# A GRU and a transformer layer in one kernel: the recurrent stage's side work dealt anew to its steps

## The chip, the core and the metric

One core of a Trainium2 chip runs the whole program. The metric is the device time of one execution in microseconds (us). Three runs of the kernel before are given with their median, and one further execution was taken by the hardware profiler.

## What is computed

```python
# x: 16 x 128 x 256 (sequences, time, width), cond: 16 x 256
def cell(h, x):                       # a GRU over 128 time steps, initial state cond
    gi = x @ W_ih + b_ih
    gh = h @ W_hh + b_hh
    r = sigmoid(i_r + h_r); z = sigmoid(i_z + h_z)
    n = tanh(i_n + r * h_n)
    return (1 - z) * n + z * h
x = x + GRU(cond, x)
# a transformer layer modulated by cond: 16 heads of 128
ada = cond @ ada_w + ada_b            # shift1, scale1, gate1, shift2, scale2, gate2
x1 = layernorm(x) * (1 + scale1) + shift1
q, k, v = split(x1 @ qkv_w + qkv_b)
attn = softmax(q k^T / sqrt(128)) v
y = x + gate1 * (attn @ out_w + out_b)
x2 = layernorm(y) * (1 + scale2) + shift2
y = y + gate2 * (gelu(x2 @ ffn_w1 + ffn_b1) @ ffn_w2 + ffn_b2)
out = x + y
```

## The kernel before

The program is written out by hand, one instruction list for each engine, with semaphores between them. It has three stages: the recurrent one (the GRU), attention over 64 pairs of a head and a group of four sequences (`d`), and the feed-forward layer. Only the recurrent stage is touched by the change.

**The recurrence.** The 128 time steps are 16 blocks `r` of 8 steps `s`. All 16 sequences go together, so a step's state is a tile of 128 x 32 (two halves of the width by 16). Each step is one chain. TensorE's `gru_step` (36 matmuls, L635 and L643) multiplies the state, kept as a float16 pair `h_hi`, `h_lo`, with `W_hh`. ScalarE makes sigmoids and a tanh (L1035 to L1040), VectorE a scan (L1318), a product (L1324), the new `h_hi` (L1330), its float32 form `hs` (L1332) and `h_lo` (L1335). The next step's matmuls wait for `h_hi`.

**The side work.** Between two steps every engine does other work, in an order fixed by tables:

- TensorE's `x_bias` and `x_products` for the next block: three matmuls for the biases (L534) and 36 input products (L547), cut over the steps by the tuple `share`: at step `s` products `share[s]` to `share[s+1]`.
- *Items* of q and k made ahead for six of the heads: an item is the q or the k of one head over two finished blocks. TensorE makes it with six matmuls of 256 columns (`ahead`, L527 to L529) in bank 4, ScalarE writes `qk_hi` (`ahead_high`, L1013), VectorE `qk_lo` (`ahead_low`, L1308). All items lie in the same columns of bank 4, so an item on TensorE waits for the `qk_lo` of the item before (`qk_l`). `PART_AT` gives the steps with an item.
- The rows of the last block, normalised and modulated: `rows_sum` (L1256) adds the state to x, TensorE turns the sum (`rows_T`, L556), VectorE does `rows_stats`, `rows_var`, `rows_scale`, `rows_shift` (L1262 to L1278) with a power on GpSimd between them (`rows_rstd`, L429), TensorE turns the rows back (`rows_back`, L563), and ScalarE and VectorE write `y_hi` and `y_lo`.
- The modulation: `row_modulation` (L568, four steps of block 0) for shift1 and scale1 and eight tiles `modulation` (L576, two float32 matmuls each, written by ScalarE at L995) for the rest, at the eight steps of block 2.
- The weights of q, k and v: SyncE loads them in pieces (`load_pieces`, 512 KB each, L331), ScalarE and GpSimd split them into float16 pairs (L1002, L423).

```python
for s in range(BS):
    gru_step(r, s)
    if s == 0 and r > 0: rows_T(r - 1)
    elif s == 5 and r > 0: rows_back(r - 1)
    x_products(r + 1, products[now[s]:now[s + 1]])
    if r == MOD_AT: modulation(G1 + s)
    if (r, s) in ITEM_AT: ahead(ITEM_AT[r, s])
```

That is TensorE's loop in short (the waits left out). On VectorE the order within a step is the five instructions of the chain, then one row operation (`row_work`), then the sum, then `ahead_low`. On ScalarE, after the tanh: the high half of x, `y_high`, the modulation tile, the pieces, and last `ahead_high`.

## Time and profile before

| what | value |
|---|---|
| median of three runs | 740.95 us (738.16 to 741.0) |
| the profiled execution's own time | 741.54 us |
| its span from the first to the last instruction | 739.7 us |
| TensorE matmul busy | 711.7 us, 96% |
| VectorE busy | 575.7 us, 78% |
| ScalarE busy | 484.0 us, 65% |
| first and last start of L1330 (`h_hi`) | 11.9 and 265.1 us |
| mean granted TensorE clock | 0.986 |

The recurrent stage is the stretch from 11.9 to 265.1 us, a little over a third of the span; attention and feed-forward fill the rest. A granted clock of 1.00 is 2.4 GHz and one of 0.50 is 1.2 GHz. In a timeline each row starts with the start of the instruction in us and its duration in us. Since L1330 stands once in each step, the distance between two of its starts is the length of a step.

### The profile page before, as it was taken

To read this page: it belongs to the slowest core of one execution; us is meant where nothing else is said; L and a number is where in the kernel's file an instruction comes from. 1 tells how busy PE (TensorE), PEld (TensorE's weight loads), DVE (VectorE), ACT (ScalarE), POOL (GpSimd) and SP (SyncE) were. 2 spreads that over 40 slices of the span, in tenths; PEclk is the share of its full clock that TensorE was granted. 3 is DMA by queue.
4 is the path that set the end of the run, shared out by engine and by line. 5 is a ranking of instruction groups with operands and counts; after the bars stand their busy time and mean duration, and the time that the engine had idled before them with its cause. 6 is when DMAs were issued, how large, how long until landed. Compare 5 with 4: busy or idle time off the path is not lost.

```text
span 739.7 us, 25163 instructions
## 1 busy us (share of the span) xinstructions
PE 711.7 (96%) x10380; PEld 525.0 (71%) x10380; DVE 575.7 (78%) x1581; ACT 484.0 (65%) x1621; POOL 104.1 (14%) x134
## 2 busy tenths in 40 slices
PE   6889999999999999999999999999999999999997
PEld 5689888888888776666767667676676777644555
DVE  5667888888888878877878988888887888834643
ACT  4346666666655567776787777877777777775453
POOL 0222222222210001011001111011110111000040
PEclk9869999999999999999999999999999999999999
DMA  6311111211000302322222332223322233200001
...
DMA packets 79017, 36.70 MB, mean 50 GB/s; under 512 B 70667, under 2 KB 73911, under 8 KB 78903
## 3 DMA queue, kind: packets, MB, share of 16 engines
...
q10 hardware_dynamic: 576, 1.57, 0.6%
q14 instruction: 32, 0.26, 0.1%
...
## 4 chain that ended last, share of the span: by engine, by line
PE 83%; DVE 6%; ACT 5%; DMA 2%; SPq 2%; issue 1%; POOL 0%; DVEq 0%; ACTq 0%
PE bank L527 20%; PE bank L529 19%; PE bank L528 19%; PE bank L635 12%; PE bank L643 5%; PE bank L547 5%; SPq L381 2%; DVE h_hi L1330 2%; ACT prob L1111 1%; PE bank L534 1%; ACT zg L1037 1%; DMA pT_lo<-p_lo 1%; DVE nu L1324 1%; DMA xr<-in_weights 1%; DVE mx L1402 1%
## 5 line engine op out<-in xcount | busy, mean ns | idle before, releaser
L635 PE MATMUL bank<-h_hi,whh_hi 128*128 128x16 f16 x1536 | 111.5, 178 | 8.6 <-DVE h_hi L1330 7.2
L635 PEld LDWEIGHTS bank<-h_hi,whh_hi 128*128 128x128 f16 x1536 | 90.0, 97 | 30.2 <-DVE h_hi L1330 26.0
L635 PE MATMUL bank<-h_hi,whh_lo 128*128 128x16 f16 x1536 | 109.9, 177 | 1.5 <-issue 1.5
L1111 ACT ACTIVATE prob<-bank,nmx 128x128 f32<-128x128 f32 x256 | 90.6, 367 | 30.7 <-DVE nmx L1405 30.4
L527 PE MATMUL bank<-y_hi,w_hi 128*128 128x256 f16 (+3 forms) x344 | 108.9, 319 | 1.0 <-DVE qk_lo L1308 0.8
L529 PE MATMUL bank<-y_lo,w_hi 128*128 128x256 f16 (+3 forms) x344 | 109.1, 319 | 0.0
L528 PE MATMUL bank<-y_hi,w_lo 128*128 128x256 f16 (+3 forms) x344 | 109.1, 319 | 0.0
L635 PEld LDWEIGHTS bank<-h_hi,whh_lo 128*128 128x128 f16 x1536 | 89.7, 96 | 1.7 <-issue 1.6
L527 PE MATMUL bank<-w_hi,y_hi 128*128 128x128 f16 x512 | 89.1, 219 | 0.6 <-DVE v_lo L1409 0.6
L528 PE MATMUL bank<-w_hi,y_lo 128*128 128x128 f16 x512 | 89.1, 219 | 0.0
L529 PE MATMUL bank<-w_lo,y_hi 128*128 128x128 f16 x512 | 89.1, 219 | 0.0
L643 PE MATMUL bank<-h_lo,whh_hi 128*128 128x16 f16 x1536 | 78.6, 178 | 0.0
L1013 ACT ACTIVATE qk_hi<-bank,small 128x256 f16<-128x256 f32 (+4 forms) x96 | 44.8, 474 | 34.2 <-PE bank L529 34.2
L1104 ACT ACTIVATE p_hi<-prob 128x512 f16<-128x512 f32 x64 | 40.4, 632 | 29.5 <-DVE prob L1419 21.5
L1446 DVE TENSOR_TENSOR four<-nat,four 128x512 f16<-128x512 f32 (+1 forms) x33 | 22.7, 689 | 44.8 <-ACT four L1147 44.7
L1035 ACT ACTIVATE zr<-bank 128x32 f32<-128x32 f32 x128 | 25.6, 200 | 48.6 <-PE bank L643 44.2
L643 PEld LDWEIGHTS bank<-h_lo,whh_hi 128*128 128x128 f16 x1536 | 56.5, 96 | 0.0
L527 PEld LDWEIGHTS bank<-w_hi,y_hi 128*128 128x128 f16 x512 | 50.1, 98 | 8.1 <-DVE v_lo L1409 1.0
L1318 DVE TENSOR_TENSOR_SCAN bank<-zr,bank 128x64 f32<-128x64 f32 x128 | 37.2, 290 | 23.2 <-ACT zr L1035 21.5
L528 PEld LDWEIGHTS bank<-w_hi,y_lo 128*128 128x128 f16 x512 | 50.1, 98 | 7.1
L1402 DVE TENSOR_REDUCE mx<-bank 128x4 f32<-128x512 f32 x64 | 44.0, 687 | 13.3 <-PE bank L529 12.6
L1413 DVE TENSOR_TENSOR p_lo<-prob,p_hi 128x512 f16<-128x512 f32 x64 | 44.2, 691 | 10.2 <-ACT p_hi L1104 7.7
...
## 6 DMA issues: line engine op xcount, KB each, us to landing
...
pT_hi<-p_hi SPq DMA_TRANSPOSE x64, 2.4
pT_lo<-p_lo SPq DMA_TRANSPOSE x64, 2.4
```

What stands on the lines that cost most here:

```text
L527: mm(ps, w[0], a[0], start=start, stop=False, skip_group_check=True)
L528: mm(ps, w[1], a[0], start=False, stop=False, skip_group_check=True)
L529: return mm(ps, w[0], a[1], start=False, stop=stop, skip_group_check=True)
L547: nc.tensor.matmul(gate_cols(n, m), w[:, k, m * P:(m + 1) * P], a[:, n % 2, k, :], start=False, stop=False, skip_group_check=True)
L635: nc.tensor.matmul(out(m0 + m), half[:, k, (m0 + m) * P:(m0 + m + 1) * P], h_hi[:, k * B:(k + 1) * B, 1], start=False, stop=False, skip_gr ...
L643: mm = nc.tensor.matmul(out(m0 + m), whh_hi[:, k, (m0 + m) * P:(m0 + m + 1) * P], h_lo[:, k * B:(k + 1) * B], start=False, stop=k == KD - ...
L1013: op = nc.scalar.activation(qk_hi[:, e, part, b, t], ps, ident_f, bias=bT[:, at:at + 1])
L1104: nc.scalar.activation(p_hi[:, :], flat_prob, copy).then_inc(p_h, 1)
L1111: op = nc.scalar.activation(prob[:, j, :], bank[3][:, j * T:(j + 1) * T], ACT.Exp, bias=nmx[:, j:j + 1], scale=SCALE, accum_out=den[:, j:j ...
L1318: nc.vector.tensor_tensor_scan(npre[r % 2].rearrange("p j s -> p (j s)"), zr[:, :, :].rearrange("p j s -> p (j s)"), n_pairs[r % 2][:, :, ...
L1402: nc.vector.reduce_max(mx[:, :], bank[3][:, :].rearrange("p (j s) -> p j s", j=QUAD), AX.X).then_inc(s_mx, 1)
L1413: tt(p_lo[:, :], flat_prob, p_hi[:, :], ALU.subtract).then_inc(p_l, 1)
```

## The change

- **Items ahead of the input products.** On TensorE an item, and a modulation tile, now stands directly behind `gru_step` (and the turned rows), ahead of `x_bias` and the products; on ScalarE `ahead_high` and the modulation tile stand ahead of the pieces. The wait for `lb_lo` is left out where an item before has had it.
- **The shares.** Blocks 3 to 14 give step 1 six products instead of nine and step 6 three instead of none. Block 1 gives 2, 12, 12, 7 and 3 products to steps 0 to 4 and none to steps 5 to 7 (before: 5, 5, 4, 5, 4, 5, 4, 4). Block 2 gives step 5 twelve instead of three and step 6 none instead of nine. Block 4 loses its seventh item, block 2 gains a second (steps 6 and 7).
- **The modulation tiles** go to steps 5 to 7 of block 1 and steps 0 to 4 of block 2. They all use bank 4. The row modulation's four matmuls move one step later (steps 4 to 7 of block 0), its additions on VectorE to step 6 of block 0 and step 0 of block 1.
- **Rows.** `rows_scale` moves from step 2 to step 1; `rows_shift` is cut into two halves of 128 columns, at steps 2 and 3; the sum is cut into three (3, 3 and 2 steps' states at steps 5, 6 and 7) instead of two (5 and 3 at steps 4 and 7).
- **Loads.** The second load of pieces waits for `z_mm` 6, the sixth step's matmuls, and the load of x for block 3 is issued ahead of it.

The diff, cut to its core:

```diff
-FIRST_R = 2
-PART_AT, PART_AT_2, PART_AT_4 = (0, 2, 3, 4, 6, 7), (7,), (0, 2, 3, 4, 5, 6, 7)
-PART_STEPS = [(r, s) for r in range(FIRST_R, NBL) for s in {2: PART_AT_2, 4: PART_AT_4}.get(r, PART_AT)]
+PART_AT = (0, 2, 3, 4, 6, 7)
+PART_STEPS = [(r, s) for r in range(2, NBL) for s in PART_AT if r > 2 or s > 5]
...
-ROW_TILES = {3: (0, 0), 4: (0, 1), 5: (1, 0), 6: (1, 1)}
+ROW_TILES = {4: (0, 0), 5: (0, 1), 6: (1, 0), 7: (1, 1)}
...
-SUMS = {4: slice(0, 5), 7: slice(5, BS)}
-MOD_AT = 2
+SUMS = {5: slice(0, 3), 6: slice(3, 6), 7: slice(6, BS)}
+MODS = [(1, 5), (1, 6), (1, 7), (2, 0), (2, 1), (2, 2), (2, 3), (2, 4)]
...
-                if r + 1 < NPR:
-                    if r > 0:
+                if r == 0:
+
+                    load_x(r + 3)
+                    sp.wait_ge(z_mm, 6)
+                    load_pieces(r + 1)
+                else:
+                    if r + 1 < NPR:
                         sp.wait_ge(piece_lo, r * PB)
-                    load_pieces(r + 1)
-                if r > 0:
-                    sp.wait_ge(xr_ok, 2 * r)
-                load_x(r + 3)
+                        load_pieces(r + 1)
+                    sp.wait_ge(xr_ok, len(SUMS) * r)
+                    load_x(r + 3)
...
-                pe.wait_ge(lb_b, n + 1)
+                pe.wait_ge(lb_b, KD * (n + 1))
...
-                        pe.wait_ge(lb_lo, t.stop // BS)
+                        if item % (2 * NA) == 0 or item >= LAST["old"]:
+                            pe.wait_ge(lb_lo, t.stop // BS)
...
-            share = (0, 0, 9, 14, 19, 24, 36, 36, 36)
-            share_2 = (0, 0, 0, 8, 16, 24, 27, 36, 36)
-            share_4 = (0, 0, 11, 16, 21, 26, 26, 31, 36)
+            share = (0, 0, 6, 11, 16, 21, 33, 36, 36)
+            share_2 = (0, 0, 0, 8, 16, 24, 36, 36, 36)
             share_0 = (0, 0, 12, 20, 23, 26, 29, 32, 36)
-            share_1 = (0, 5, 10, 14, 19, 23, 28, 32, 36)
+            share_1 = (0, 2, 14, 26, 33, 36, 36, 36, 36)
             for r in range(NBL):
-                now = {0: share_0, 1: share_1, 2: share_2, 4: share_4}.get(r, share)
+                now = {0: share_0, 1: share_1, 2: share_2}.get(r, share)
                 for s in range(BS):
                     gru_step(r, s)
                     if s == 0 and r > 0:
                         if r == 1:
-                            pe.wait_ge(rows_ok, 2)
+                            pe.wait_ge(rows_ok, 1)
                         rows_T(r - 1)
                     elif s == 5 and r > 0:
                         rows_back(r - 1)
+                    if (r, s) in ITEM_AT:
+                        if ITEM_AT[r, s] == 0:
+                            pe.wait_ge(ada_add, len(MODS))
+                        ahead(ITEM_AT[r, s])
+                    elif (r, s) in MODS:
+                        i = MODS.index((r, s))
+                        if i == 0:
+                            pe.wait_ge(rest_in, 16)
+                            pe.wait_ge(rows_ok, 2)
+                        else:
+                            pe.wait_ge(ada_add, i)
+                        modulation(G1 + i)
                     if r < NBL - 1:
                         if s == (1 if r > 1 else 0):
                             x_bias(r + 1)
                         elif s == 1 and r == 0:
                             pe.wait_ge(xt_lo, 2)
                         x_products(r + 1, products[now[s]:now[s + 1]])
-                    if r == MOD_AT:
-                        if s == 0:
-                            pe.wait_ge(rest_in, 16)
-                        elif s == BS - 1:
-                            pe.wait_ge(lb_lo, r)
-                        else:
-                            pe.wait_ge(ada_add, s)
-                        modulation(G1 + s)
-                    if r == NBL - 1:
+                    else:
                         if s == 1:
                             pe.wait_ge(piece_lo, NPIECE)
                             pe.wait_ge(lb_lo, NBL - 2)
                         for i in range(tall_at[s], tall_at[s + 1]):
                             tall_parts(tall_rest[i % 6:i % 6 + 1], WHOLE[0], i // 6, early)
-                    if (r, s) in ITEM_AT:
-                        if ITEM_AT[r, s] == 0:
-                            pe.wait_ge(ada_add, ADA - G1 - 1)
-                        ahead(ITEM_AT[r, s])
                     if r == 0 and s in ROW_TILES:
-                        if s == 3:
+                        if s == min(ROW_TILES):
                             pe.wait_ge(adaw_in, 48)
                         row_modulation(*ROW_TILES[s])
...
-                    if r == MOD_AT:
-                        modulation_out(G1 + s)
+                    if (r, s) in ITEM_AT:
+                        ahead_high(ITEM_AT[r, s])
+                    elif (r, s) in MODS:
+                        modulation_out(G1 + MODS.index((r, s)))
                     if r < NPR:
                         pieces = (1, 2, 2, 2, 3, 4, 4, 4) if r > 0 else (0, 0, 0, 0, 1, 2, 3, 4)
                         for i in range(pieces[s - 1] if s else 0, pieces[s]):
                             piece_high(r * PB + i)
-                    if (r, s) in ITEM_AT:
-                        ahead_high(ITEM_AT[r, s])
...
-                dve.wait_ge(lb_ag, n + 1)
                 dve.wait_ge(rows_ok, 2)
                 stt(ra[:, :], row_ps, mvb[:, 0:1], scale_rows[:, :], ALU.subtract, ALU.mult).then_inc(lb_a, 1)
 
-            def rows_shift(n):
-                dve.wait_ge(lb_a, n + 1)
-                dve.wait_ge(lb_r, n + 1)
-                stt(rb[:, :], ra[:, :], rsb[:, :], shift_rows[:, :], ALU.mult, ALU.add).then_inc(lb_b, 1)
+            def rows_shift(n, k):
+                if k == 0:
+                    dve.wait_ge(lb_r, n + 1)
+                    dve.wait_ge(lb_a, n + 1)
+                c = slice(k * P, (k + 1) * P)
+                stt(rb[:, c], ra[:, c], rsb[:, :], shift_rows[:, c], ALU.mult, ALU.add).then_inc(lb_b, 1)
...
-                    if r > 0 and s in row_work:
-                        row_work[s](r - 1)
+                    if r > 0:
+                        row_work(r - 1, s)
                     if r == 0 and s == 0:
                         x_low(1)
                     if s in SUMS:
                         rows_sum(r, SUMS[s])
                     if (r, s) in ITEM_AT:
                         ahead_low(ITEM_AT[r, s])
-                    if r == 0 and s in (5, 7):
-                        row_modulation(s // 6)
+                    if (r, s) in ((0, 6), (1, 0)):
+                        row_modulation(r)
                     elif r == NBL - 1 and s == 7:
                         modulation_gates()
```

Three places in the order of the instructions. **First TensorE**, step 3 of block 8, from the last matmuls of `gru_step` on. Before:

```order
L643 MATMUL bank<-h_lo,whh_hi 128x16 x4
L547 MATMUL bank<-xb_lo,wih_hi 128x128
L547 MATMUL bank<-xb_hi,wih_hi 128x128
L547 MATMUL bank<-xb_hi,wih_lo 128x128
L547 MATMUL bank<-xb_lo,wih_hi 128x128
L547 MATMUL bank<-xb_hi,wih_hi 128x128
L527 MATMUL bank<-y_hi,w_hi 128x256 [waits qk_l,lb_lo]
L528 MATMUL bank<-y_hi,w_lo 128x256
L529 MATMUL bank<-y_lo,w_hi 128x256
```

and now:

```order
L641 MATMUL bank<-h_lo,whh_hi 128x16 x4
L526 MATMUL bank<-y_hi,w_hi 128x256 [waits qk_l]
L527 MATMUL bank<-y_hi,w_lo 128x256
L528 MATMUL bank<-y_lo,w_hi 128x256
L526 MATMUL bank<-y_hi,w_hi 128x256
L527 MATMUL bank<-y_hi,w_lo 128x256
L528 MATMUL bank<-y_lo,w_hi 128x256
L546 MATMUL bank<-xb_lo,wih_hi 128x128
L546 MATMUL bank<-xb_hi,wih_hi 128x128
```

The item, which waits for `qk_l`, has gone ahead of the five products, so they are queued behind its wait.

**Then VectorE**, steps 2 and 3 of block 8, from `h_lo` of step 2 on. Before:

```order
L1335 TENSOR_TENSOR h_lo<-hs,h_hi 128x32 [waits h32_ok]
L1273 SCALAR_TENSOR_TENSOR ra<-bank,mvb,scale_rows 128x256 [waits rows_ok,lb_ag]
L1308 SCALAR_TENSOR_TENSOR qk_lo<-bank,small,qk_hi 128x16x16 [waits qk_h]
L1318 SCALAR_TENSOR_TENSOR bank<-zr,bank 128x64 [waits hn_mm,r_ok]
L1324 TENSOR_TENSOR nu<-zg,hs 128x32 [waits z_ok]
L1330 SCALAR_TENSOR_TENSOR h_hi<-zz,nu 128x64 [waits nu_ok]
L1332 SCALAR_TENSOR_TENSOR hs<-zz,nu 128x64
L1335 TENSOR_TENSOR h_lo<-hs,h_hi 128x32 [waits h32_ok]
L1278 SCALAR_TENSOR_TENSOR rb<-ra,rsb,shift_rows 128x256 [waits lb_r,lb_a]
L1308 SCALAR_TENSOR_TENSOR qk_lo<-bank,small,qk_hi 128x16x16 [waits qk_h]
```

and now:

```order
L1344 TENSOR_TENSOR h_lo<-hs,h_hi 128x32 [waits h32_ok]
L1276 SCALAR_TENSOR_TENSOR rb<-ra,rsb,shift_rows 128x128 [waits lb_a,lb_r]
L1306 SCALAR_TENSOR_TENSOR qk_lo<-bank,small,qk_hi 128x16x16 [waits qk_h]
L1327 SCALAR_TENSOR_TENSOR bank<-zr,bank 128x64 [waits hn_mm,r_ok]
L1333 TENSOR_TENSOR nu<-zg,hs 128x32 [waits z_ok]
L1339 SCALAR_TENSOR_TENSOR h_hi<-zz,nu 128x64 [waits nu_ok]
L1341 SCALAR_TENSOR_TENSOR hs<-zz,nu 128x64
L1344 TENSOR_TENSOR h_lo<-hs,h_hi 128x32 [waits h32_ok]
L1276 SCALAR_TENSOR_TENSOR rb<-ra,rsb,shift_rows 128x128
L1306 SCALAR_TENSOR_TENSOR qk_lo<-bank,small,qk_hi 128x16x16 [waits qk_h]
```

Of the two whole row operations ahead of `qk_lo` the first has left this stretch (it stands in step 1 now), and the second has become two halves, one in each step.

**Last SyncE's queue**, from the first load of pieces on. Before:

```order
L331 DMA stage<-in_weights 128x1024
L328 DMA x<-in_x 128x256
L331 DMA stage<-in_weights 128x1024
L328 DMA x<-in_x 128x256
L351 DMA xr<-in_ada_r 128x2x1024 [waits rows_mm,whh_l,wih_l]
L331 DMA stage<-in_weights 128x1024 [waits piece_lo]
```

and now:

```order
L326 DMA stage<-in_weights 128x1024
L323 DMA x<-in_x 128x256 x2
L326 DMA stage<-in_weights 128x1024 [waits z_mm]
L346 DMA xr<-in_ada_r 128x2x1024 [waits rows_mm,whh_l,wih_l]
L326 DMA stage<-in_weights 128x1024 [waits piece_lo]
```

The second load of pieces has moved behind both loads of x and waits for the sixth step.

## Rows read from the trace of the kernel before

**Rows 1.** Stretches: block 2, then ahead of and inside its half clock. Columns: length; busy times of PE, PEld, DVE, ACT, POOL; granted clock, DMA share, GB/s.
```profile
43.00:61.60 18.60, 18.29 (x366) 17.48 (x367) 11.53 (x49) 8.30 (x46) 4.00 (x6) 0.63 0.14 38
...
40.50:43.70 3.20, 1.98 (x62) 1.64 (x58) 2.27 (x11) 0.95 (x7) 0.81 (x2) 1.00 0.00 0
43.90:57.40 13.50, 13.50 (x251) 12.78 (x248) 7.79 (x32) 5.68 (x32) 2.66 (x4) 0.50 0.18 51
```

**Rows 2.** VectorE's timeline in block 8, steps 1 to 6.
```profile
143.93 0.29 DVE L1330 TENSOR_TENSOR_SCAN h_hi<-zz,nu 128x64 f16<-128x64 f32 x1
...
145.96 0.29 DVE L1330 TENSOR_TENSOR_SCAN h_hi<-zz,nu 128x64 f16<-128x64 f32 x1
...
146.97 0.48 DVE L1308 SCALAR_TENSOR_TENSOR qk_lo<-bank,small,qk_hi 128x256 f16<-128x256 f32 x1
...
147.91 0.29 DVE L1330 TENSOR_TENSOR_SCAN h_hi<-zz,nu 128x64 f16<-128x64 f32 x1
...
148.53 0.48 DVE L1278 SCALAR_TENSOR_TENSOR rb<-ra,rsb,shift_rows 128x256 f32<-128x256 f32 x1
148.96 0.48 DVE L1308 SCALAR_TENSOR_TENSOR qk_lo<-bank,small,qk_hi 128x256 f16<-128x256 f32 x1
...
149.91 0.29 DVE L1330 TENSOR_TENSOR_SCAN h_hi<-zz,nu 128x64 f16<-128x64 f32 x1
...
151.90 0.29 DVE L1330 TENSOR_TENSOR_SCAN h_hi<-zz,nu 128x64 f16<-128x64 f32 x1
...
153.82 0.29 DVE L1330 TENSOR_TENSOR_SCAN h_hi<-zz,nu 128x64 f16<-128x64 f32 x1
```

**Rows 3.** VectorE's timeline, the same instruction in blocks 0 to 3.
```profile
17.62 0.29 DVE L1330 TENSOR_TENSOR_SCAN h_hi<-zz,nu 128x64 f16<-128x64 f32 x1
...
23.45 0.29 DVE L1330 TENSOR_TENSOR_SCAN h_hi<-zz,nu 128x64 f16<-128x64 f32 x1
...
29.20 0.29 DVE L1330 TENSOR_TENSOR_SCAN h_hi<-zz,nu 128x64 f16<-128x64 f32 x1
31.33 0.29 DVE L1330 TENSOR_TENSOR_SCAN h_hi<-zz,nu 128x64 f16<-128x64 f32 x1
...
44.92 0.29 DVE L1330 TENSOR_TENSOR_SCAN h_hi<-zz,nu 128x64 f16<-128x64 f32 x1
...
57.70 0.29 DVE L1330 TENSOR_TENSOR_SCAN h_hi<-zz,nu 128x64 f16<-128x64 f32 x1
...
63.65 0.29 DVE L1330 TENSOR_TENSOR_SCAN h_hi<-zz,nu 128x64 f16<-128x64 f32 x1
```

**Rows 4.** TensorE's timeline, weight loads in step 4 of block 0.
```profile
19.86 0.10 PEld L635 LDWEIGHTS bank<-h_hi,whh_lo 128*128 128x128 f16 x1 [1.56 <-issue]
```

**Rows 5.** DMA queues from 17.4 to 17.6 us: packets, MB, share of 16 engines.
```profile
q8 instruction: 1, 0.02, 30.2%
```

**Rows 6.** DMA queues from 13.7 to 17.4 us: the only row.
```profile
q1 hardware_dynamic: 518, 1.13, 78.8%
```

**Rows 7.** TensorE's timeline in step 3 of block 8 and the start of step 4.
```profile
147.24 0.22 PE L547 MATMUL bank<-xb_lo,wih_hi 128*128 128x128 f16 x1
...
147.46 0.22 PE L547 MATMUL bank<-xb_hi,wih_hi 128*128 128x128 f16 x1
147.59 0.27 PE L527 MATMUL bank<-y_hi,w_hi 128*128 128x256 f16 x1
...
148.14 0.27 PE L529 MATMUL bank<-y_lo,w_hi 128*128 128x256 f16 x1
148.26 0.19 PE L635 MATMUL bank<-h_hi,whh_hi 128*128 128x16 f16 x1
```

**Rows 8.** ScalarE's timeline, the high half of that item.
```profile
148.45 0.47 ACT L1013 ACTIVATE qk_hi<-bank,small 128x256 f16<-128x256 f32 x1 [0.56 <-PE bank L529]
```

**Rows 9.** Timelines of VectorE and TensorE behind the last step of block 15.
```profile
268.80 0.60 DVE L1308 SCALAR_TENSOR_TENSOR qk_lo<-bank,small,qk_hi 128x128 f16<-128x128 f32 x2
...
268.94 0.44 PE L563 MATMUL bank<-ident,rb 128*128 128x128 f32 x2 [0.93 <-DVE rb L1278]
```

25 lines of the change are left out of this document (15 added, 10 removed).

## The prediction

> **What bounds the kernel now.** I read the stretches first: block 2 takes 18.60 us at a mean granted clock of 0.63, and inside it TensorE is busy 13.50 of 13.50 us at half clock [rows 1]. Then VectorE's timeline, whose `h_hi` rows are the beat of the recurrence. The quietest beat of block 8 is its last one shown, 153.82 - 151.90 = 1.92 us [rows 2]. I take 1.92 as the chain's own length, which nothing the change moves can shorten; side work only adds to it. Block 8 has 2.03 for step 2, 1.95 for step 3, 2.00 and 1.99 for steps 4 and 5 [rows 2]: 0.29 above four quiet beats. In block 0 steps 4 and 5 together take 5.83, step 1 of block 1 takes 2.13, the five beats from 44.92 to 57.70 take 12.78, and the three behind them 5.95 [rows 3]. The whole stage holds 265.1 - 11.9 - 127 x 1.92 = 9.4 us above its quiet beats. That is all the change can win; behind the end of block 15 the program is the same.
>
> **The change part by part**, against the profiled execution's own 741.54 us.
>
> *Steps 4 and 5 of block 0*: 5.83 is 1.99 above two quiet beats. TensorE sat 1.56 us in the middle of step 4's matmuls for "issue", that is, for nothing the trace shows [rows 4]. The queue that carries instructions moved a packet only between 17.4 and 17.6 us [rows 5]. From 13.7 until then it moved none, and data packets kept the DMA engines busy for 78.8% [rows 6]; the second load of pieces, 0.5 MB, is among the 1.13 MB of that row. At the row's rate, 1.13 MB in 3.7 us, 0.5 MB is 1.6 us, as long as the wait. The change takes that load out of the stretch, so I take the wait as gone, and the slower fifth step with it, since the clock fell just behind the pause: -1.99, bounds -1.99 and 0. The load comes back in step 6. Its first pieces are split in block 1, over 6 us later, so nobody waits.
> Against this stands the Trainium skill, "DMA: Bandwidth & Descriptors", section "Queues, rings and completion order": each DMA engine takes turns between its queues packet by packet. By that rule a fetch on a queue of its own isn't held up by how much lies on the data queue; the wait would stay and the sum be 1.99 higher. That is rival B.
>
> *Block 1.* Step 1's beat of 2.13 comes from step 0's side work on TensorE: turned rows, biases and five products. It has two now: -0.2. The twelve products in steps 1 and 2 cost 12 x 0.055 = 0.66 (a product each 0.055: 147.24 to 147.46 is four [rows 7]). The recurrent matmuls take 0.93 (their successor starts at 147.24, 1.28 behind `h_hi`, and they start 0.35 behind it, as 148.26 behind 147.91 [rows 2, 7]). 1.59 is under 1.92, so the chain hides them: 0. The same chain hides the row modulation in its new steps: 0, and under 0.1 each if it doesn't.
>
> *Block 2.* Steps 0 to 4 keep their TensorE work: a modulation tile each, biases in step 1, eight products from step 2 on. Ahead of the half clock, from 40.5 to 43.7, the engine was busy 1.98 of 3.20 us [rows 1]. The change makes the steps there emptier still, so I take the half clock to come again and last as long: 0. Step 5 has twelve products for three. At half clock nine more at 0.11 (twice 0.055) are 1.0, less 0.2 of slack: +0.8. At full clock they are 0. The clock rose in this very step, so I take +0.1. Step 6 gives its nine products up and step 7 its modulation tile, which stood ahead of an item; with them goes what the three beats behind 57.70 have above 5.76: -0.19.
>
> *Blocks 3 to 14.* Three products fewer in step 1 are 0.17, more than the 0.11 that step 2's beat has over: -0.11. `rows_scale` leaves step 2, which frees VectorE for the scan: -0.03. Now steps 3 and 4, where the order matters. In step 3 the item's first matmul started at 147.59 [rows 7], 0.14 behind the end of step 2's `qk_lo` (146.97 + 0.48 [rows 2]). The five products before it were over at 147.51, so they filled the wait. Now they are queued behind it. How early can `qk_lo` be? The row operation starts 0.62 behind `h_hi` (148.53 - 147.91) and a whole one takes 0.43 to the next start (148.96 [rows 2]). A half shift is not in the trace: its price lies between nothing and 0.43. Two 128-column operations of its kind take 0.60 together, one whole one of 0.34 behind a start 0.26 later [rows 9]; it is nearest to these, and I take 0.27. So `qk_lo` starts at 0.89 and ends at 1.37, the item starts at 1.51, takes 0.66 (its first five gaps 0.55, 147.59 to 148.14) and the products 0.27: 2.44. The next step's matmuls are due at 1.92 + 0.35 = 2.27, so they are 0.17 late. In the following step ScalarE's half starts 0.31 behind the item's last matmul and `qk_lo` 0.51 behind that (148.14, 148.45, 148.96 [rows 2, 7, 8]); the same count gives another 0.07. Beats 4 and 5 become 2.09 and 1.99, for 2.00 and 1.99: +0.09. Sum per block -0.05; twelve blocks: -0.6. Block 4 also loses its seventh item, with an estimated 0.1 (its steps as dense as steps 3 and 4): -0.1. Block 15 has no products: 0. In steps 6 and 7 an item with three products is 0.93 + 0.66 + 0.17 = 1.76, under 1.92: 0. On ScalarE the piece now stands behind the item's half, in what was idle time (0.56 ahead of L1013 [rows 8]): 0, and under 0.1 in one step of a block if that cover is gone.
>
> *The end.* Turning the last rows back waited 0.93 for the shift [rows 9]. Two halves end 0.27 + 0.34 = 0.61 behind their start, one whole 0.48: +0.13.
>
> Sum: -1.99 - 0.2 + 0.1 - 0.19 - 0.6 - 0.1 + 0.13 = -2.85, so 738.7 on the profiled execution's basis. The median of the runs is 0.59 below it: **738.1**.
>
> **The rivals.**
>
> *A. The waits ahead of the items don't bite.* If `qk_lo` is done when the recurrent matmuls end, beats 4 and 5 are 1.92 too, which takes off 0.24 in thirteen blocks, 3.1: 735.0. For it speaks that the margin rests on a price no row shows. Against it, that even a shift of no length leaves 0.62 + 0.48 + 0.14 = 1.24 for the item's start, just the end of the recurrent matmuls.
>
> *B. The wait in block 0 stays.* 738.1 + 1.99 = 740.1. For it: the fetch is one packet, and its latency may be its own. Against: it moved just as the data ran out.
>
> *C. The clock stays up in block 2.* The five beats lose 12.78 - 9.60 = 3.18, and the +0.1 goes: 734.8. For it: steps 1 and 2 of block 1 get twelve products each, which may carry the clock over. Against: the emptiest steps come right behind. The Trainium skill, "TensorE: Matmul & The Clock Gate", section "HAM oscillation", ties a fall to the engine waiting idle between bursts, and by that rule a stage with matmuls in every step would keep its clock. The trace doesn't agree: the clock went from 1.00 to 0.50 between 43.7 and 43.9 us [rows 1] with matmuls in every step.
>
> *D. The half clock spreads: slower than before.* It would have to fall ahead of block 1 and stay to the end of block 2. Priced with side work at twice its length: four row modulations, each at most the 0.43 that steps 4 and 5 of block 0 have above the idle row, 1.7; block 1's step 0 +1.0 (1.2 of side work less three products, doubled, less slack); its twelve-product steps 0.93 + 1.32 = 2.25, 0.33 each; step 5 of block 2 +0.7; its item steps 0.33 each. Sum 4.7: 742.8. It decides from the point where an emptied step of block 0 (three products in step 3, no row modulation) is enough to drop the clock.
>
> **How the numbers follow.** My forecast 0.48, A 0.20, B 0.16, C 0.07, D 0.09. A measurement of this kernel can tell 0.5%, 3.7 us, from no change, so the bounds are 737.2 and 744.7. Faster: A, C and a quarter of my own case, 0.39. Slower: the part of D that also meets the full-priced half shift or the wait of block 0, 0.06. Same: 0.55. The range goes down to C's 734.8, and up to B with the half shift at 0.43 (0.16 later in step 3 of some ten blocks, 1.7): 741.8.
>
> **What would show it.** In the changed profile: no "issue" wait over 0.5 us in block 0 (else B). Beats in blocks 3 to 14 of 1.92 for step 2, about 2.1 for step 4 and 2.0 for step 5, with the item's first matmul 0.14 behind the end of `qk_lo` (1.92 in all would be A). Beats of 2.6 in block 2 at a clock of 0.50 (else C), and none in blocks 0 and 1 (else D). The last `h_hi` near 262.2 us instead of 265.1. A rest behind it that differs by over 0.5 us, or a new wait for a load in block 1, would make the prediction wrong where I did not look.

## The result, and the profile after

The changed kernel takes 744.43 us (median of 8 runs, 742.28 to 745.66), the one before 740.84 us, measured beside it (8 runs, 737.37 to 742.42): ratio 1.0054, interval 1.0036 to 1.0071. It is 3.6 us slower where 2.9 us less was forecast, and above the range, which ended at 741.8. A second comparison later gave 744.47 against 740.64, ratio 1.0061 (1.0039 to 1.0083).

The page of the changed kernel: span, busy times, and the shares of the chain that ended last.
```profile
span 743.6 us, 25117 instructions
PE 713.2 (96%) x10380; PEld 531.7 (72%) x10380; DVE 581.7 (78%) x1613; ACT 478.8 (64%) x1621; POOL 103.5 (14%) x134
...
PE bank L526 19%; PE bank L528 18%; PE bank L527 18%; PE bank L633 11%; PE bank L641 5%; DMA pT_lo<-p_lo 4%; PE bank L546 4%; DVE h_hi L1339 2%; SPq L380 2%; ACT prob L1108 1%; PE bank L533 1%; ACT zg L1034 1%; DVE nu L1333 1%; DVE mx L1411 1%; PE bank L573 1%
```
The last `h_hi` on VectorE's timeline, the kernel before first, then the changed one.
```profile
265.12 0.29 DVE L1330 TENSOR_TENSOR_SCAN h_hi<-zz,nu 128x64 f16<-128x64 f32 x1
```
```profile
263.81 0.29 DVE L1339 TENSOR_TENSOR_SCAN h_hi<-zz,nu 128x64 f16<-128x64 f32 x1
```
So the recurrent stage, the only one that the change touches, ends 1.3 us **earlier**. The loss lies behind it: 739.7 - 265.1 = 474.6 us before, 743.6 - 263.8 = 479.8 us now, 5.2 us more in a part whose program is word for word the same. Something there is new in the chain of waits, the transfer `pT_lo<-p_lo` with 4% of the span (it had 1%). This is the DMA transpose of the low halves of the probabilities, one a head, 64 in all. TensorE's own waits for it, before and after:
```profile
PE bank L527 <- DMA pT_lo<-p_lo: 1.0, 4, 0.3
```
```profile
PE bank L526 <- DMA pT_lo<-p_lo: 6.0, 8, 1.1
```
One of the eight is head 39. SyncE's timeline has both kernels issue this transpose at almost the same time, before and then after:
```profile
511.37 1.20 SPq L381 DMA_TRANSPOSE pT_lo<-p_lo  x1
```
```profile
511.26 1.19 SPq L380 DMA_TRANSPOSE pT_lo<-p_lo  x1
```
The view of DMA queues and issues over that transpose, before (511.3 to 513.9 us) and after (511.2 to 515.3). The last number of the issue is the us to landing.
```profile
q1 hardware_dynamic: 697, 0.16, 32.0%
q14 instruction: 1, 0.01, 0.9%
...
pT_lo<-p_lo SPq DMA_TRANSPOSE x1, 2.4
```
```profile
q1 hardware_dynamic: 825, 0.20, 51.6%
q8 instruction: 1, 0.02, 2.0%
...
pT_lo<-p_lo SPq DMA_TRANSPOSE x1, 4.0
```
In the changed kernel a packet on queue q8 moves while the transpose is on its way, and none does in the kernel before. q8 is the queue of rows 5. That it carries TensorE's instructions is read from the count: 82 packets of 16 KB in a run for some 20,940 instructions, one for every 256. The packet starts 1.16 us behind the start of the transpose's issue; in the kernel before the nearest one had started 1.97 ahead of it. In the changed kernel TensorE then waits 1.12 us, the longest of its waits above:
```profile
515.29 0.23 PE L526 MATMUL bank<-pT_hi,v_hi 128*128 128x128 f16 x1 [1.12 <-DMA pT_lo<-p_lo]
```
The clock has no part in it: behind the recurrent stage both traces record a granted clock of 1.00 throughout.

The stretch of half clock ran from 43.9 to 57.4 us before [rows 1]. It is shown here for the changed kernel, and with it a shorter one that the kernel before had in block 1 as well and the changed one does not:
```profile
41.40:58.50 17.10, 17.10 (x302) 16.21 (x298) 10.42 (x44) 7.36 (x40) 3.47 (x6) 0.50 0.14 41
```
```profile
33.60:37.00 3.40, 3.09 (x81) 2.71 (x81) 2.56 (x11) 1.02 (x8) 0.67 (x1) 0.50 0.16 57
```
The columns of both are those of rows 1.

VectorE's timeline of block 8, which answers to rows 2, with the row of GpSimd's timeline for the same time in the middle. (The sum of the states into x is `xr<-x,hs`.)
```profile
143.52 0.29 DVE L1339 TENSOR_TENSOR_SCAN h_hi<-zz,nu 128x64 f16<-128x64 f32 x1
145.44 0.29 DVE L1339 TENSOR_TENSOR_SCAN h_hi<-zz,nu 128x64 f16<-128x64 f32 x1
...
146.32 0.48 DVE L1306 SCALAR_TENSOR_TENSOR qk_lo<-bank,small,qk_hi 128x256 f16<-128x256 f32 x1
...
147.36 0.29 DVE L1339 TENSOR_TENSOR_SCAN h_hi<-zz,nu 128x64 f16<-128x64 f32 x1
149.35 0.29 DVE L1339 TENSOR_TENSOR_SCAN h_hi<-zz,nu 128x64 f16<-128x64 f32 x1
151.26 0.29 DVE L1339 TENSOR_TENSOR_SCAN h_hi<-zz,nu 128x64 f16<-128x64 f32 x1
```
```profile
152.11 0.67 POOL L422 TENSOR_TENSOR w_lo<-stage,w_hi 128x256 f16<-128x256 f32 x1 [1.25 <-DVE h_lo L1344]
```
```profile
152.22 0.71 DVE L1253 TENSOR_TENSOR xr<-x,hs 128x96 f32<-128x96 f32 x1
153.40 0.29 DVE L1339 TENSOR_TENSOR_SCAN h_hi<-zz,nu 128x64 f16<-128x64 f32 x1 [0.18 <-ACT nu L1037]
154.02 0.29 DVE L1253 TENSOR_TENSOR xr<-x,hs 128x96 f32<-128x96 f32 x1
155.32 0.29 DVE L1339 TENSOR_TENSOR_SCAN h_hi<-zz,nu 128x64 f16<-128x64 f32 x1
```
The beats of steps 2 to 7 of block 8 take 1.92, 1.92, 1.99, 1.91, 2.14 and 1.92 us (the beat of a step ends with its `h_hi`, so it holds the side work of the step before). The slow one is step 6: the sum of three states behind step 5 took 0.71 us, the same sum one step later 0.29. Beside the first, GpSimd lowered a piece of weights.

In block 0, TensorE's timeline (weight loads) has in place of the 1.56 us of rows 4:
```profile
19.18 0.10 PEld L633 LDWEIGHTS bank<-h_hi,whh_lo 128*128 128x128 f16 x1 [0.76 <-issue]
```
And the end, which answers to rows 9:
```profile
267.04 0.61 DVE L1276 SCALAR_TENSOR_TENSOR rb<-ra,rsb,shift_rows 128x128 f32<-128x128 f32 x2 [0.27 <-POOL rsb L428]
...
267.71 0.44 PE L560 MATMUL bank<-ident,rb 128*128 128x128 f32 x2 [0.99 <-DVE rb L1276]
```

### The profile page after: what moved, and what is told of

Its sections match the earlier page's. It is cut to its first block, busy times and chain, and to the rows that moved or that the text cites. A ratio compares the mean times of both kernels' runs of the same rounds, so it can differ in the third digit from the quotient of the medians.

```text
span 743.6 us, 25117 instructions
## 1 busy us (share of the span) xinstructions
PE 713.2 (96%) x10380; PEld 531.7 (72%) x10380; DVE 581.7 (78%) x1613; ACT 478.8 (64%) x1621; POOL 103.5 (14%) x134
## 3 DMA queue, kind: packets, MB, share of 16 engines
q1 hardware_dynamic: 78327, 33.53, 20.5%
## 4 chain that ended last, share of the span: by engine, by line
PE 78%; DVE 8%; DMA 5%; ACT 5%; issue 2%; SPq 2%; POOL 0%; DVEq 0%; ACTq 0%
PE bank L526 19%; PE bank L528 18%; PE bank L527 18%; PE bank L633 11%; PE bank L641 5%; DMA pT_lo<-p_lo 4%; PE bank L546 4%; DVE h_hi L1339 2%; SPq L380 2%; ACT prob L1108 1%; PE bank L533 1%; ACT zg L1034 1%; DVE nu L1333 1%; DVE mx L1411 1%; PE bank L573 1%
## 5 line engine op out<-in xcount | busy, mean ns | idle before, releaser
L1101 ACT ACTIVATE p_hi<-prob 128x512 f16<-128x512 f32 x64 | 40.4, 632 | 37.2 <-DVE prob L1428 19.9
L1108 ACT ACTIVATION_READ_ACCUMULATOR prob<-bank,nmx 128x1 f32 x256 | 52.2, 204 | 0.0
```

Source lines behind the costliest of these rows:

```text
L1101: nc.scalar.activation(p_hi[:, :], flat_prob, copy).then_inc(p_h, 1)
L1108: op = nc.scalar.activation(prob[:, j, :], bank[3][:, j * T:(j + 1) * T], ACT.Exp, bias=nmx[:, j:j + 1], scale=SCALE, accum_out=den[:, j:j ...
```

## The experiments

Two theories for the 5.2 us. **P**: an instruction fetch that falls into a DMA transpose delays it, and the change has shifted the fetches. TensorE's program has 181 separate wait instructions now and had 243, because an item no longer waits for `lb_lo` where an item before has done so. All else on TensorE is equal in number, so behind the stage each fetch stands at another place relative to the transposes, by 62 of the 256 instructions. **R**: something else of the change (its tail, for one). "Stage" is the time of the last `h_hi` of the profiled run, "rest" its span less that; each is read from one execution. Each ratio is to runs of the kernel before measured beside it, whose median lay between 739.64 and 740.84 us.

| kernel | waits on TensorE | stage | rest | median us | ratio to before (95%) |
|---|---|---|---|---|---|
| before | 243 | 265.1 | 474.6 | 740.84 | 1 |
| changed | 181 | 263.8 | 479.8 | 744.43 | 1.0054 (1.0036 to 1.0071) |
| changed, again | 181 | 263.6 | 481.6 | 744.47 | 1.0061 (1.0039 to 1.0083) |
| after_itemwaits | 243 | 264.9 | 474.1 | 741.03 | 1.0010 (0.9998 to 1.0022) |
| before_fewwaits | 181 | 262.9 | 479.1 | 743.14 | 1.0042 (1.0026 to 1.0059) |
| after_pad30 | 211 | 263.6 | 475.6 | 742.18 | 1.0027 (1.0014 to 1.0041) |
| before_pad66 | 309 | 265.6 | 481.4 | 746.27 | 1.0086 (1.0067 to 1.0104) |
| before_loads | 243 | 263.3 | 473.8 | 739.32 | 0.9987 (0.9974 to 0.9999) |
| after_sums67 | 181 | 260.2 | 480.6 | 742.04 | 1.0023 (1.0011 to 1.0036) |
| after_pool467 | 181 | 259.9 | 479.3 | 743.27 | 1.0053 (1.0032 to 1.0074) |
| after_piece6 | 181 | 262.9 | 478.1 | 743.21 | 1.0042 (1.0030 to 1.0055) |
| after_piece3 | 181 | 263.0 | 481.3 | 744.62 | 1.0065 (1.0047 to 1.0084) |
| after_xfirst | 181 | 262.5 | 480.4 | 745.36 | 1.0072 (1.0060 to 1.0085) |
| sums67_pad69 | 249 | 266.5 | 474.6 | 743.21 | 1.0041 (1.0025 to 1.0057) |
| sums67_fill38 | 181 + 76 | 261.4 | 473.5 | 736.99 | 0.9955 (0.9942 to 0.9968) |
| fill38_share | 181 + 76 | 260.9 | 475.1 | 736.88 | 0.9959 (0.9946 to 0.9972) |
| fill38_late | 181 + 76 | 257.6 | 473.5 | **733.29** | 0.9911 (0.9898 to 0.9924) |
| before_fill | 181 + 76 | 261.1 | 473.4 | 736.03 | 0.9944 (0.9924 to 0.9964) |

("+ 76" are the instructions of 38 filler matmuls.)

### Where the fetches fall

**after_itemwaits** and **before_fewwaits** exchange one condition between the two kernels, in the function that issues an item on TensorE:
```diff
 # after_itemwaits takes it out of the changed kernel, before_fewwaits puts it into the one before
-                        if item % (2 * NA) == 0 or item >= LAST["old"]:
-                            pe.wait_ge(lb_lo, t.stop // BS)
+                        pe.wait_ge(lb_lo, t.stop // BS)
```


> The changed kernel with the wait for lb_lo again ahead of every item, as before the change: 62 wait instructions more on TensorE (243 instead of 181), all in the recurrent stage; nothing computed differently. Theory P (place of the instruction fetches): the 16 KB fetches of TensorE's instructions come every 256 instructions, and in the changed kernel they fall about 62 instructions earlier in the program's order relative to the DMA transposes of the probabilities than before; a fetch that starts 1 to 2 us into the transpose of p_lo makes it land after 4.0 to 4.2 us and not 2.4. With the 62 instructions back, the rest behind the recurrent stage is 474.6 us again (479.8 now) and the whole about 739.3 us. Rival R (the rest is longer by something else of the change: its tail, its order on VectorE, a shifted clock): the rest stays at 479.8 and the whole at 744.4, or 0.2 more for the waits.

> The kernel before, with only the condition of the change on the wait for lb_lo ahead of the items: 62 wait instructions fewer on TensorE (181 instead of 243). Theory P: the rest behind the recurrent stage goes from 474.6 to about 479.8 us, and the whole from 740.8 to about 746 us, though nothing but satisfied waits is taken away. Rival R: nothing happens, 740.8 us or up to 0.5 less.

Rest 474.1 and 479.1: P holds, in both directions, within 0.7 us, and R, which expected 479.8 and 474.6, falls. Every wait that comes or goes stands behind an earlier wait for the same thing, and none is behind the stage. The wholes moved less than expected: 741.03 for 739.3, and 743.14 for 746, which is 3.0 us above the 740.19 of the kernel before beside it. The waits cost something in the stage as well. after_itemwaits has 2.07 and 1.99 us in the beats of steps 4 and 5 for 1.99 and 1.92, 1.7 us over blocks 3 to 14; before_fewwaits gains 1.2 us there. Another 0.7 and 0.9 us of the stages' differences lie in block 0, where the wait of rows 4 is of another length in every execution. The view of the tile `pT_lo`, first of before_fewwaits, then of after_itemwaits: who waited for it (us in total, times), and its 64 transposes' time to landing.
```profile
  ACT p_hi L1105: 15.5, 13
  PEld bank L527: 11.6, 16
...
DMA to landing us min/median/max: 2.4/2.5/4.0
```
```profile
  ACT p_hi L1100: 5.7, 8
  PEld bank L526: 3.9, 10
...
DMA to landing us min/median/max: 2.4/2.4/3.8
```
**after_pad30** and **before_pad66** add satisfied waits, spread over blocks 2 to 15 (n = 30 and 66; the count goes up by one in n of the 112 steps):
```diff
+                    for i in range(n * (step + 1) // 112 - n * step // 112 if r >= 2 else 0):
+                        pe.wait_ge((lb_lo, lb_b)[i], 1)
                     gru_step(r, s)
```


> The changed kernel with 30 satisfied waits more on TensorE, spread one at a time over the steps of blocks 2 to 15. Theory P: the fetches move by half of the way; counted over the 64 transposes of the trace, weighted lateness falls from 32 to 26 us (after_itemwaits: 15), so that the rest would be near 478 us and the whole near 742.6. A theory that it is the waits at the items themselves that matter (they hold TensorE back at a better moment) expects 744.4 here. Rival R: 744.4.

> The kernel before with 66 satisfied waits MORE on TensorE, one at a time over the steps of blocks 2 to 15 (309 wait instructions; the changed kernel has 181, the one before 243). It asks whether the number matters only as a place within the 256 instructions of a fetch, or because fewer waits are bad. Theory P: 128 more than the changed kernel puts each fetch on the transposes of the other heads, at nearly the same place in them, so the rest behind the stage is long again (lateness 26 of 32): near 478.5 us, and with 0.1 to 0.15 us a block for the waits the whole is near 745 us. A theory that waits on TensorE help the rest (more waits, shorter rest) expects the rest at 474.6 or less and the whole near 741.5.

30 more give a rest between the two, 475.6; lower than the 478 expected, and the whole went where it should (742.18 for 742.6). 66 more than before make the rest long again, 481.4 (478.5 expected), and the whole 746.27 (745 expected). So it isn't the number of waits, which runs 181, 243, 309 while the rest runs 480, 474, 481: it is the place within a fetch's period, as P says and as no other theory here does. The 64 transposes follow each other every 128 of TensorE's instructions on average, half a period, so a shift by 128 brings the fetches back to the same places.

The collision itself can be read over the traces of all 18 kernels and runs: 1134 transposes of `p_lo` (all but the first of each trace), sorted by when the nearest packet of q8 started, counted from the start of the transpose's issue.

| fetch starts | issue takes, median | lands after, median | number |
|---|---|---|---|
| none from 1.0 us ahead to 2.3 behind | 1.22 | 2.45 | 869 |
| 0.4 ahead to 0.8 behind | 2.05 | 3.26 | 146 |
| 0.8 to 1.2 behind | 1.22 | 3.58 | 33 |
| 1.2 to 2.0 behind | 1.22 | 4.00 | 57 |

(29 lie between these rows.) A transpose with no fetch near it takes 2.45 us, 9 in 10 of them between 2.43 and 2.46; 16 KB of instructions that start in its first 2 us add 0.8 to 1.6. Of the 869, 23 took over 2.6 us, and none of these was alone: four had a packet of q8 2.4 to 2.5 us behind (4.4 to 4.5 us), and 19 one of 8 KB on the other instruction queue, q14. Where that one started 1.9 to 2.1 behind the start of the issue, in 14 transposes of 14 traces, the transpose took 3.3 to 3.4 us; where it started 0.4 to 1.0 behind, 2.4 to 2.7. Added up over the heads, `p_lo` lands 24 to 29 us late in the kernels with 181 or 309 waits, 16 with 211, and 3 to 9 with 243 to 257. That a fetch which hits the transpose of `p_hi` instead costs little, because most of its delay is over before `p_lo` lands, is my reading and not shown. The rest goes in step with these sums: 478.1 to 481.6, 475.6, 473.4 to 475.1.

### What a wait instruction costs

> The changed kernel with the sums at steps 6 and 7 (5 and 3 states) and 68 to 69 satisfied waits more on TensorE, put where it is idle by the trace for 0.18 us or more a beat (steps 0, 1, 2 and 7 of blocks 2 to 15, all of block 1, the last five of block 0). Theories P and S together: stage as in after_sums67 (steady beats 1.92, 15.42 a block), the rest near 473.5 us (lateness 11 of 32), the whole near 736 us, which is under both kernels. If the waits cost their 0.02 to 0.03 us there too, 737.5. Rival (two effects do not add): 739 or more.

The rest is near the forecast, 474.6 for 473.5, and the stage is not: 266.5 us, 6 more than after_sums67, and the whole, 743.21 for 736, lies where the rival had put it (739 or more). The two effects don't simply add, because the waits that move the fetches have a price of their own: 5.1 us of the 6 lie in blocks 3 to 15, and 1.4 in block 2, whose half clock was longer. `h_hi` in block 8, in steps that had idle time:
```profile
141.80 0.29 DVE L1341 TENSOR_TENSOR_SCAN h_hi<-zz,nu 128x64 f16<-128x64 f32 x1
143.78 0.29 DVE L1341 TENSOR_TENSOR_SCAN h_hi<-zz,nu 128x64 f16<-128x64 f32 x1
145.77 0.29 DVE L1341 TENSOR_TENSOR_SCAN h_hi<-zz,nu 128x64 f16<-128x64 f32 x1
147.69 0.29 DVE L1341 TENSOR_TENSOR_SCAN h_hi<-zz,nu 128x64 f16<-128x64 f32 x1
```
1.98 and 1.99 us where a wait was added, 1.92 where not. A satisfied wait directly ahead of the recurrent matmuls costs 0.06 to 0.07 us a beat though TensorE was idle there. My reading, argued and not tested: it makes the wait for `h_hi` an instruction of its own too, and the matmul starts only behind that. So moving the fetches with waits is a poor tool; the next kernels do it with matmuls.

### The sum at step 5

> The changed kernel with the sum of a block's states in two pieces at steps 6 and 7 (5 and 3 states), in place of three at steps 5, 6 and 7. Theory S: the 0.22 to 0.3 us more of the seventh beat of blocks 1, 3 and 5 to 11 (and 6 of block 0) come from the sum of three states at step 5, which takes 0.71 us while GpSimd works on the low halves of a piece of weights beside it and 0.29 us where GpSimd rests; without it these beats are 1.92 us, the stage is 2.2 to 2.6 us shorter and the whole about 742.0 us, if the rest stays. Rival: the sum of five states at step 6 is as much in the way of its scan; the beat of step 7 takes the excess and the whole stays at 744.4.

```diff
-SUMS = {5: slice(0, 3), 6: slice(3, 6), 7: slice(6, BS)}
+SUMS = {6: slice(0, 5), 7: slice(5, BS)}
```
The beat of step 6 is 1.92 in all blocks, and a block of the changed kernel that took 15.64 takes 15.42. The whole is 742.04, as expected. The sum of five states, now at step 6, takes 0.45 us and has started before GpSimd's operation. Whether it is GpSimd or a crowded step that makes the sum slow, the next kernels ask.

> The changed kernel with the fourth piece of weights of a block converted in step 6 and not in step 5 (on ScalarE, and GpSimd's low half behind it); the sums stay at steps 5, 6 and 7. Theory S (the sum is slow because GpSimd works on a piece beside it, wherever that is): the sum at step 5 takes 0.29 us and the one at step 6 0.7, the beat of 2.14 us moves from the seventh place of a block to the eighth, and the time stays at 744.4 within 0.6. Rival (step 5 is too full for VectorE: y_low and a sum ahead of the scan, whoever works beside it): the beat stays at the seventh place. Third: step 6 has no y_low, so the slow sum may fit there, and both beats are 1.92: 2 us less, 742.4.

> The changed kernel with the third piece of weights of a block converted in step 3 and not in step 4. In after_piece6 the moved piece was the wrong one: GpSimd's half that runs beside the sum of step 5 is the third piece's (152.11 to 152.78 us in block 8 of the changed kernel's trace), one step behind ScalarE's. Theory S: GpSimd now works on it in step 4, the sum of step 5 has VectorE's port to itself and takes 0.29 us, the seventh beat is 1.92 in all blocks, the stage is 2.0 us shorter and the whole near 742.4 (against 744.4). Rival (step 5 is too full for VectorE whoever works beside it): 744.4.

> The changed kernel once more, unchanged, beside the others of this call: all theories expect the ratio of the first comparison, 1.0054 within 0.002, and the rest behind the stage near 480 us in the profiled execution. It is the base that after_piece3 is read against, and shows how far the half clock and the rest move from one execution to the next.

```diff
 # n = 6: (1, 2, 2, 2, 3, 3, 4, 4); n = 3: (1, 2, 2, 3, 3, 4, 4, 4)
-                        pieces = (1, 2, 2, 2, 3, 4, 4, 4) if r > 0 else (0, 0, 0, 0, 1, 2, 3, 4)
```
Both missed their aim. They move ScalarE's step, and GpSimd has step numbers of its own: it stayed where it was, the sum took 0.72 us and the beat 2.14 in both. They say nothing on the question. The third moves GpSimd:
```diff
-                    piece_low(r * PB + i, t0 + 5 + i + late)
+                    piece_low(r * PB + i, t0 + 5 + i + (1 if i else 0) + late)
```


> The changed kernel with GpSimd's own step numbers moved: it makes the low halves of a block's pieces behind steps 4, 6 and 7 and not 4, 5 and 6 (after_piece6 and after_piece3 moved ScalarE's step, which GpSimd does not follow: it waits for a given h_lo). Theory S: beside the sum of step 5 GpSimd now rests, the sum takes 0.29 us, the seventh beat 1.92, the stage is 2.0 us shorter, and with the fetches where they are the whole is near 742.4. In steps 6 and 7 GpSimd starts 0.85 us behind h_hi and the sum ends 0.9 behind it, so they hardly meet. Rival (step 5 is too full for VectorE whoever works beside it): sum 0.29 or 0.71, beat still 2.14, 744.4.

VectorE's timeline, block 8:
```profile
149.10 0.29 DVE L1253 TENSOR_TENSOR xr<-x,hs 128x96 f32<-128x96 f32 x1
150.07 0.29 DVE L1339 TENSOR_TENSOR_SCAN h_hi<-zz,nu 128x64 f16<-128x64 f32 x1
150.69 0.29 DVE L1253 TENSOR_TENSOR xr<-x,hs 128x96 f32<-128x96 f32 x1
151.99 0.29 DVE L1339 TENSOR_TENSOR_SCAN h_hi<-zz,nu 128x64 f16<-128x64 f32 x1
```
The sum stays where it was, takes 0.29 us, and the beat is 1.92: GpSimd was the cause. The trace of the changed kernel has it too: 152.11 + 0.67 = 152.78 ends GpSimd's operation, and the sum that "started" at 152.22 ended 0.15 behind that. The Trainium skill, "SBUF — State Buffer", section "SBUF: two separate sides", has the rule: an operation of VectorE with two inputs in SBUF and one of GpSimd that reads SBUF exclude each other for a whole instruction. By that rule `qk_lo`, one of whose inputs is in PSUM, isn't blocked. The trace agrees: in block 8 of the changed kernel it starts 0.13 us behind GpSimd's operation and takes its usual 0.48.
```profile
142.44 0.67 POOL L422 TENSOR_TENSOR w_lo<-stage,w_hi 128x256 f16<-128x256 f32 x1 [3.17 <-DVE h_lo L1344]
142.57 0.48 DVE L1306 SCALAR_TENSOR_TENSOR qk_lo<-bank,small,qk_hi 128x256 f16<-128x256 f32 x1
```
The lock works the other way round as well, and that stood in the trace of the kernel before: where the sum of five states (0.45 us) had started 0.23 us ahead, GpSimd's operation took 0.76 us and not 0.67 (at 150.75 us in block 8, and likewise in blocks 3 to 11).

The whole of after_pool467 is 743.27 with runs from 741.08 to 744.74, and the interval of its ratio holds the changed kernel's; the 2 us are shown in the stage, not in the medians.

### Loads, and the order on TensorE

> The kernel before with the order of the loads in block 0 alone taken from the change (first x, then, behind z_mm 6, the pieces of weights). It asks what the later loads alone are worth. The prediction put it at -1.9 to -2.0 us: the fourth beat of block 0 from 3.59 to 1.92 and the fifth from 2.24 to 1.92. The trace of the changed kernel shows a fourth beat of 2.74 (2.4 to 2.75 in four runs with these loads, 3.0 and 3.6 in two without), so the expectation now is -0.5 to -1.0 us: about 739.5 us. Rival: nothing, because the fetch comes as late with them.

```diff
+                if r == 0:
+                    load_x(r + 3)
+                    sp.wait_ge(z_mm, 6)
+                    load_pieces(r + 1)
```
1.0 us less (739.32 against 740.30 beside it; the interval of the ratio ends just under 1). The beat of step 4 of block 0 is 2.39 us. Over all traces it lies from 1.92 to 3.45 with the later loads (median 2.5 of 14) and from 2.78 to 3.59 without (3.0 of 4): shorter, and gone in four traces only. The wait follows the fetch: in the 13 traces that have one here, it stands ahead of the same instruction of TensorE, the 450th of the matmuls and weight loads, whatever was added ahead of it, and in all 18 traces this instruction comes 2.2 to 2.6 us behind the start of the packet of q8. The packet starts at 17.0 to 17.5 us in the four kernels with the early load and at 15.7 to 17.2 (median 16.7) in the others. So the load was worth about half a microsecond of it.

> The changed kernel with the input products ahead of the item again in every step, as before the change; the shares, the waits and their number stay (181 wait instructions, so the fetches stay where they are). Theory I (the item at the head waits for qk_lo): in the trace of the changed kernel the item of step 3 starts 0.08 us after TensorE is free, because its wait for the low halves of the item before ends then, and the fifth beat of blocks 3 to 14 is 1.99 us; with five products (0.27 us) ahead of it that wait is hidden, the beat is 1.92, and the whole is about 0.9 us shorter, 743.5. Rival J (the item first is what shortens the beats 3 and 4, as the change has it): they go back to 2.03 and 1.95 and the whole is 1.0 to 1.5 us longer, near 745.6.

The beats of steps 3, 4 and 5 are 1.95, 1.92 and 1.95 in place of 1.92, 1.99 and 1.92. The sum is the same: a wait that goes from one step turns up in the next ones. The whole, 745.36, isn't told apart from 744.43 by the intervals. Both theories fall; the order on TensorE is worth nothing either way that these runs can tell.

> sums67_fill38 with two input products moved from step 3 to step 6 (shares 0, 6, 5, 3, 5, 12, 5, 0 in place of 0, 6, 5, 5, 5, 12, 3, 0). If TensorE's work in step 3 sets the fifth beat (1.99 us), it falls to 1.92 in blocks 3 to 14 and the whole by 0.9 us to about 736.1. If the wait for qk_lo alone set it, nothing changes: 737.0.

Nothing again (736.88 for 736.99): the 1.99 us went from step 4 to step 5.

### Fillers, and the clock

```diff
+            FILL = ((5, 1, 3, 3, 3, 3, 3, 3), (1, 1, 1, 4, 6, 1, 0, 0))
+            def filler(r, n):
+                for _ in range(n):
+                    nc.tensor.matmul(r_bank[(r + 1) % 2][:, 256:512], wih_hi[:, 0, 0:P], wih_hi[:, 0, 0:256], start=True, stop=True, skip_group_check=True)
...
+                    if r < 2:
+                        filler(r, FILL[r][s])
```


> The changed kernel with the sums at steps 6 and 7 and 38 filler matmuls of 128x256 (into unused columns of the next block's bank; they compute nothing that is read) in the idle time of TensorE in blocks 0 and 1: 76 instructions, so the place of the fetches is about that of sums67_pad69. It asks what the half clock of block 2 costs and whether more work on TensorE before it keeps the clock up. Theory C (low use of TensorE in blocks 0 and 1 is what is answered with half a clock): the stretch of 13.7 to 17.1 us at half clock is gone or shorter, block 2 lasts 15.5 us in place of 18.0 to 19.6, and the whole is 2.5 us or more below sums67_pad69, near 733.5. Rival: the stretch stays as it is and the whole equals sums67_pad69 within 0.5.

736.99 us, under the kernel before by 0.45% (0.32 to 0.58): the fetches are in a good place, rest 473.5, and nothing was paid for it in the steady beats. The clock fell all the same, for 13.7 us. The 733.5 that theory C expected did not come, and it isn't the rival's sums67_pad69 either, whose waits have their own price. So the fillers went where it falls:
```diff
-            FILL = ((5, 1, 3, 3, 3, 3, 3, 3), (1, 1, 1, 4, 6, 1, 0, 0))
+            FILL = ((0, 0, 0, 0, 0, 1, 2, 2), (1, 1, 2, 4, 6, 3, 3, 3), (2, 2, 2, 2, 2, 0, 0, 0))
```


> sums67_fill38 with its 38 filler matmuls later: 5 in block 0, 23 in block 1 (3 in each of its last three steps), 10 in the first five steps of block 2. The fetches behind the stage stay where they are. Theory C again, in its stronger form (it is the little work of the last steps of block 1 and the first of block 2 that is answered with half a clock): the stretch at half clock is gone or starts later and is shorter, block 2 goes from 18.7 us towards 16, less up to 0.2 us a step for the fillers. Rival: the clock falls at the same place for as long, and the fillers, which take twice as long at half clock, cost 1 us or more in block 2: 738 or more.

Stretches of fill38_late, the steps ahead of block 2 and then the place of the half clock:
```profile
38.50:44.00 5.50, 5.38 (x127) 4.52 (x124) 4.14 (x18) 2.86 (x16) 1.20 (x2) 1.00 0.01 3
43.40:59.40 16.00, 15.73 (x375) 14.12 (x373) 12.42 (x53) 8.69 (x45) 4.05 (x6) 1.00 0.15 45
```
The same first stretch of sums67_fill38 and of the kernel before:
```profile
38.50:44.00 5.50, 4.60 (x120) 4.37 (x120) 4.09 (x18) 2.79 (x16) 1.42 (x2) 0.84 0.01 3
```
```profile
38.50:44.00 5.50, 3.99 (x120) 3.46 (x117) 4.01 (x17) 2.11 (x13) 1.65 (x3) 0.98 0.02 3
```
The clock stays at 1.00, block 2 lasts 15.9 us for 18.7, and the whole is 733.29, with the same number of instructions as sums67_fill38 and fill38_share: 3.6 us under the 736.88 of fill38_share, measured beside it, of which 3.1 are block 2 by the traces. It beats both kernels, 0.9% under the one before (0.76 to 1.02).

> The kernel before with its 62 waits less (as before_fewwaits) and the 38 late filler matmuls of fill38_late: the same place of the fetches as in the fastest kernel, the clock kept up if the fillers do it here too, and nothing else of the change. It tells what the change itself (order, shares, halves, loads) is worth where neither the fetches nor the clock speak in it. From before_fewwaits: stage 262.9 less 2.5 to 3 for block 2, rest 473.5, so near 735.3 us, 2 us above fill38_late. If the clock falls all the same, 738.

736.03: the clock stays up here as well over block 2 (16.0 us). Against fill38_late it is 2.7 us slower (2.4 by the ratios, whose intervals just touch). Of the 3.4 us between the stages, 1.5 lie in blocks 3 to 14, 0.13 a block, and are the change's own, with the sums moved; another 1.5 lie in and ahead of block 0 and differ from run to run. The change's parts do pay once fetches and clock leave them alone.

## Why the prediction was wrong, point by point

**"Behind the end of block 15 the program is the same."** This is the step that failed. I priced the rest at nothing, because it is the same program; it took 5.2 us more, from 474.6 to 479.8. The prediction named a rest that differs by over 0.5 us as a sign that it would be wrong where it did not look, and gave it no price and no chance. The two kernels that exchange only the waits show it without anything else of the change. The trace of before had the means to see it: rows 5 and 6 are about a 16 KB fetch beside data, and I took it for a matter of block 0. Its own transposes of `p_lo` land late by 8.6 us in all. The 62 waits that the change takes out stand nowhere in the sum, neither as cost (1.2 to 1.7 us in the stage by these two kernels) nor as length of the program.

**Steps 4 and 5 of block 0, -1.99.** Half right. The wait was 0.76 us in place of 1.56 and the two beats 4.70 in place of 5.83: -1.1. In before_loads the loads alone gave -1.0 us of the median. The step that failed here is the size: 0.5 MB at the row's rate were to be 1.6 us, and the fetch came 0.55 us earlier (16.92 for 17.47), about as much as between the two groups of traces above. Rival B, that the wait stays whole, did not come in this trace; but after_again kept more than half of it (a beat of 2.97), and after_piece6, with the same loads, nearly all (1.44 us, and 5.69 for 5.83 in the two beats):
```profile
19.50 0.10 PEld L633 LDWEIGHTS bank<-h_hi,whh_lo 128*128 128x128 f16 x1 [1.44 <-issue]
```
The wait is set by when the fetch starts, and how far the load sets that differs from run to run.

**Block 1, -0.2.** -0.21 in step 1, given back in step 6 (2.14).

**Block 2, half clock of the same length.** It came again, as forecast, and lasted 17.1 us for 13.5, with the beat of step 6, which holds step 5's twelve products, at 2.70 for 1.92: +0.8. That is the very figure that the prediction worked out for half clock (1.0 less 0.2) and then took as +0.1, because the clock had risen in that step before. The beats of steps 3 to 5 are 2.67 for 2.59, another +0.24 that it had at nothing. The length isn't the change's alone: with the 3.4 us in block 1 the kernel before had 17.0 us of half clock in blocks 1 and 2, and added up so it is 10.2 to 20.5 us in ten traces of the changed kernel and its variants without fillers, and 10.2 to 17.1 in four of the kernel before and its variants. Rival C was priced right (3.2; block 2 of fill38_late is 3.1 us shorter than that of fill38_share) and needed work in the last steps of block 1, which the change doesn't put there. Rival D didn't come: in both kernels the clock is down for 3.4 us around step 5 of block 0 (19.9 and 21.0 us on) and rises again.

**Blocks 3 to 14, steps 2 and 3.** -0.12 and -0.04 for -0.11 and -0.03.

**Steps 4 and 5: 2.09 and 1.99.** They were 1.99 and 1.91. The half shift was right: `qk_lo` started 0.88 behind `h_hi` (0.89) and ended at 1.36 (1.37). But the item started 0.05 behind that, and not 0.14:
```profile
146.85 0.28 PE L526 MATMUL bank<-y_hi,w_hi 128*128 128x256 f16 x1
```
I had read 0.14 off a place where the item stood behind products, in which that was their end and not a wait. Rival A came half true: beat 5 was 1.91, beat 4 was not 1.92.

**Step 6: under 1.92.** 2.24 in block 0 and 2.14 in blocks 1, 3 and 5 to 11, the term that I didn't have: 0.32 + 9 x 0.22 = 2.3 us. I let three states of sum pass as hidden and never asked who works beside them. after_pool467 shows that it was GpSimd.

**The end, +0.13.** +0.08 from the last `h_hi` to the turning of the rows (3.90 for 3.82), and the wait 0.99 for 0.93.

The stage was forecast to end near 262.2 and ended at 263.8; the sum beside GpSimd (2.3), what stayed of the wait in block 0 (0.9) and block 2 at half clock (0.9) stand against 1.8 that steps 4 and 5 did better and some 0.7 of small gains. The rest turned the sign.
